# Router exponentials of the last two sequences as powers on GpSimd, and Silu for every expert block

## The chip, the cores and the metric

The kernel runs on one core of a Trainium2 chip. The metric is the device time of one execution in microseconds (us), the median over several runs.

## The reference

The input `x` is 32 sequences of 256 tokens with 128 features. The reference computes an attention layer (16 heads of 64, causal softmax, output projection), adds the input and normalises. Then comes a mixture of 8 experts:

```
xn     = layernorm(x) * gamma + beta
probs  = softmax(xn @ router_w.T / 1.5)        # 8 experts
w, idx = top_k(probs, 2)
h      = silu(xn @ W1[e])                      # 128 -> 512, for the two chosen experts
y      = h @ W2[e]                             # 512 -> 128
out    = layernorm(x + sum over the two of w * y)
```

All of it is float32. `silu(z)` is `z * sigmoid(z)`, which is also `0.5 * z * (tanh(z / 2) + 1)`.

## The kernel before

Each engine has one program, written out by hand in order; an engine takes up an instruction only when the one before it has been taken up, and semaphores join the engines. There is no planner: what is written first runs first.

*Attention* runs in 32 x 4 steps (`step(n, q, d)`; four quads of heads for each sequence). The products with split weights are three matmuls each, with a rounded high part and a low part. During sequence n the kernel also finishes sequence n - 1: projection, residual, norm (on GpSimd, with powers of -0.5 for the square roots, L586 and L597), then the router. One router call is: logits on TensorE, `router_difference` on VectorE (minus the maximum, L1174 and L1176), `router_exponentials` on ScalarE (L804), `router` on VectorE (sum, top 8, index, gates, `chosen`, L1107 to L1137), `ranks` on TensorE, `places` on VectorE, `slots` on GpSimd, and `send_tokens`, four indirect writes of the token rows into a queue in HBM sorted by expert (L639). The calls are numbered 2 to 33. The last two, 32 and 33, no longer fall into attention but among the first expert blocks.

*The experts* run over `NJ` = 71 blocks of 256 queued rows. For block j the SyncE queue loads the rows (`m_x`), TensorE transposes them (L1523), ScalarE applies gamma and beta (`affine`, L887) and rounds (`m_xhi`, L890), VectorE makes the low part (`m_xlo`, L1302), TensorE does the first layer (`hidden`, L1424, into two halves of PSUM), the activation function is applied, TensorE does the second layer (`output`, L1718), VectorE weights the result (`rows`, L1312, two blocks later), and GpSimd writes it to `y_tok` in HBM with two indirect writes (L742). There are 4 buffers for results: `rows(j)` waits until the writes of block j - 4 have landed.

The order within block j on each engine is:

- TensorE: transposes of block j + 1, first layer of block j, extra work (block 4: logits of router 33; block 2: ranks of router 32; block 7: ranks of router 33), second layer of block j - 1.
- ScalarE: `affine(j + 1)`, the two halves of the activation function, the copy of the weights of block j + 2 (L901, L903).
- VectorE: `rows(j - 2)`, `destinations(j)` (five small operations and `m_keep`; L1271 to L1294), `m_xlo` of block j + 1, extra work (block 0: `router(32)`; block 4: `router_difference(33)`; block 6: `router(33)`).
- GpSimd: results of sequence 32 first (norm, slots, `send_tokens`), then the two writes of each block; `slots(33)` and its four queue writes stand in front of block 9.

In blocks 0 to 5 (`SILU_FROM` = 6) ScalarE makes Tanh of half the hidden value, and VectorE makes `(tanh + 1) * z` from it (L1360); the missing factor 0.5 is in the gates. From block 6 on ScalarE makes Silu in one instruction. Tanh and Exp are in one activation table; Silu is in another, and the one load stands in front of block 6's first Silu.

Of the kernel before, what the change touches and what calls it, by code (L numbers as in the profile page):

```python
# [1 line left out]

# [8 lines left out]
ALU = mybir.AluOpType  # L11
# [3 lines left out]
P = 128  # L15
# [7 lines left out]
ROWS = BLOCKS * P  # L23
WBUFS = 4
LATER = 71
SILU_FROM = 6
FBUFS = 6
EARLY = 11
FIRST_LOAD, LOAD_EVERY = 37, 3
# [6 lines left out]
def postln_block(nc, x, wq, wk, wv, bq, bk, bv, wo, bo, gamma, beta, router_wt, w1, w2, out):  # L36
# [37 lines left out]
    with ExitStack() as ctx:  # L74
        def sb(name, shape, dt=F32):
            return ctx.enter_context(nc.sbuf_tensor(name, shape, dt))
# [4 lines left out]
        def sem(name):  # L81
            return ctx.enter_context(nc.semaphore(name))
# [87 lines left out]
        r_negmax = sb("r_negmax", [P, TILES])  # L170
        r_diff = sb("r_diff", [P, TILES, E])
        r_exp = sb("r_exp", [P, TILES, E])
        r_sum = sb("r_sum", [P, TILES])
        r_inv = sb("r_inv", [P, TILES])
        r_top = sb("r_top", [P, TILES, E])
# [46 lines left out]
        m_w2 = sb("m_w2", [P, E * HID])  # L222
        m_xhi = sb("m_xhi", [P, 2, ROWS], F32R)
        m_xlo = sb("m_xlo", [P, 2, ROWS], F32R)
        m_tanh = [early_use[:, at * HD:at * HD + CH * ROWS].rearrange("p (c t) -> p c t", c=CH) for at in (9, 15)]
        m_h = early_use[:, 10 * HD:10 * HD + 2 * CH * ROWS].rearrange("p (a c t) -> p a c t", a=2, c=CH)
        m_xf = early_use[:, 12 * HD:12 * HD + 2 * ROWS].rearrange("p (a t) -> p a t", a=2)
        m_y = early_use[:, 14 * HD:14 * HD + YBUFS * ROWS].rearrange("p (a b d) -> p a b d", a=YBUFS, b=BLOCKS)
# [114 lines left out]
        m_xnt_done = sem("m_xnt_done")  # L343
        m_xhi_done = sem("m_xhi_done")
        m_xlo_done = sem("m_xlo_done")
        m_tanh_done = sem("m_tanh_done")
        m_h_done = sem("m_h_done")
        m_silu_done = sem("m_silu_done")
        m_rows_done = sem("m_rows_done")
        m_second_done = sem("m_second_done")  # L350
# [56 lines left out]

        def wait_units(engine, j, half):

            if j < SILU_FROM:  # L410
                engine.wait_ge(m_h_done, j * 2 + half + 1)
            else:
                engine.wait_ge(m_silu_done, (j - SILU_FROM) * 2 + half + 1)

        def f_sum(f):

# [112 lines left out]
        def _(pool):  # L529
# [7 lines left out]
            for par in range(2):  # L537
                pool.iota(z[:, par, :, TOK], [[P, TILES]], base=(par - 2) * S, channel_multiplier=1,
                          allow_small_or_imprecise_dtypes=True)
            pool.memset(eps_sb[:], EPS)  # L540
            pool.memset(neg_half[:], -0.5)
            pool.memset(neg_one[:], -1.0)
            pool.memset(neg_two[:], -2.0)
# [104 lines left out]
            def residual_input(n):  # L648
# [5 lines left out]
                    ins = pool.tensor_tensor(xb[:, i, :], x_raw[:, (n - 1) % 2, i, :], bo_sb[:], ALU.add)  # L654
                ins.then_inc(xb_done, 1)

            def round_outputs(s):
                m, first = s // QUADS, s % QUADS * 2
                pool.wait_ge(ot_done, s + 1)
                if m >= 1:  # L660
                    pool.wait_ge(out_half_ready, 2 * m - (1 if first < 4 else 0))
                pool.tensor_copy(ot_hi[:, first:first + 2, :], ot[:, s % 2]).then_inc(ot_hi_done, 1)  # L662
# [42 lines left out]
            for s in range(LAST - 2, LAST):  # L705
                round_outputs(s)
                rest_of_outputs(s)
            residual_input(SEQS)
            send_tokens(SEQS - 1, 1)
            norm(SEQS)  # L710
            slots(SEQS)
# [18 lines left out]
            for j in range(NJ):  # L730
                if LATER <= j + 2 < NJ:
                    rest_of_expert_weights(j + 2)
                if j == 9:
                    slots(SEQS + 1)
                    for i in range(TILES):
                        send_tokens(SEQS + 1, i)
                if j - 2 in load_at[:EARLY]:
                    piece_power(load_at.index(j - 2))
                pool.wait_ge(m_dest_done, j + 1)
                pool.wait_ge(m_rows_done, j + 1)  # L740
                for i in range(BLOCKS):
                    pool.indirect_dma_start(  # L742
                        y_tok, bass.IndirectOffsetOnAxis(ap=m_dest[:, j % (2 * YBUFS), i:i + 1], axis=0),
                        m_y[:, j % YBUFS, i, :], None, bounds_check=TOP * TOKENS - 1, oob_is_err=False
                    ).then_inc(m_y_sent[j % YBUFS], 16)
# [11 lines left out]
        def _(act):  # L757
# [146 lines left out]
                ins.then_inc(m_w_hi_done, 1)  # L904

            affine(0)
            copy_outputs(LAST - 2)
            first_pt(LAST)
            expert_weights(0)
            copy_outputs(LAST - 1)  # L910
            expert_weights(1)
            router_exponentials(SEQS)
            for j in range(NJ):
                if 1 <= j < NJ - 1:
                    affine(j + 1)
                for half in range(2):
                    act.wait_ge(m_z_ready, j * 2 + half + 1)
                    if j < SILU_FROM:
                        act.activation(m_tanh[j % 2][:, 2 * half:2 * half + 2, :], hidden_at(j, half), ACT.Tanh, scale=0.5
                                       ).then_inc(m_tanh_done, 1)  # L920
                    else:
                        act.activation(m_h[:, j % 2, 2 * half:2 * half + 2, :], hidden_at(j, half), ACT.Silu
                                       ).then_inc(m_silu_done, 1)
                if j == 0:
                    affine(1)
                if j + 2 < NJ:
                    expert_weights(j + 2)
                if j == 1:
                    copy_projection(SEQS)
                if j == 3:  # L930
                    act.wait_ge(zt_ready, SEQS)
                    act.activation(xnt[:], ps_f[:, 0:S], ACT.Identity, scale=gamma_sb[:, 0:1],
                                   bias=beta_sb[:, 0:1]).then_inc(xnt_done, 1)
                if j == 5:
                    router_exponentials(SEQS + 1)

            for f in range(FINS - EARLY):
                act.wait_ge(f_shift_done, f + 1)
# [7 lines left out]
        def _(dve):  # L946
# [321 lines left out]
            def destinations(j):  # L1268
                dve.wait_ge(m_x_loaded[j % WBUFS], (j // WBUFS + 1) * 16)
                line = m_x[:, j % WBUFS]  # L1270
                dve.scalar_tensor_tensor(out=m_second[:, j % 2, :], in0=line[:, :, SLOT], scalar=t_row[:, j:j + 1],  # L1271
                                         in1=row_no[:], op0=ALU.subtract, op1=ALU.is_equal
                                         ).then_inc(m_second_done, 1)
                dve.wait_ge(m_second_done, j + 1)
                if j >= 2 * YBUFS:
                    dve.wait_ge(m_y_sent[j % YBUFS], (j // YBUFS - 1) * BLOCKS * 16)
                dve.scalar_tensor_tensor(out=m_dest[:, j % (2 * YBUFS), :], in0=m_second[:, j % 2, :], scalar=float(TOKENS),  # L1277
                                         in1=line[:, :, TOK], op0=ALU.mult, op1=ALU.add).then_inc(m_dest_done, 1)
                dve.scalar_tensor_tensor(out=m_scale[:, j % 2, :], in0=m_second[:, j % 2, :], scalar=1.0,
                                         in1=line[:, :, KEEP], op0=ALU.subtract, op1=ALU.mult  # L1280
                                         ).then_inc(m_scale_done, 1)
                if j < SILU_FROM:
                    dve.scalar_tensor_tensor(out=m_extra[:, j % 2, :], in0=m_second[:, j % 2, :], scalar=0.5,
                                             in1=line[:, :, MORE], op0=ALU.mult, op1=ALU.mult).then_inc(m_extra_done, 1)
                else:
                    dve.tensor_tensor(m_extra[:, j % 2, :], m_second[:, j % 2, :], line[:, :, MORE], ALU.mult
                                      ).then_inc(m_extra_done, 1)
                dve.wait_ge(m_scale_done, j + 1)
                for i in range(BLOCKS):
                    ins = dve.tensor_scalar(m_keep[:, j % 3, i, :], line[:, i, 0:D], m_scale[:, j % 2, i:i + 1], None,  # L1290
                                            ALU.mult)
                ins.then_inc(m_keep_done, 1)
                dve.wait_ge(m_extra_done, j + 1)
                dve.scalar_tensor_tensor(out=m_gate[:, j % 4, :], in0=line[:, :, GATE],  # L1294
                                         scalar=0.5 if j < SILU_FROM else 1.0, in1=m_extra[:, j % 2, :],
                                         op0=ALU.mult, op1=ALU.add).then_inc(m_gate_done, 1)

            def rest_of_x(j):
                dve.wait_ge(m_xhi_done, j + 1)
# [50 lines left out]
            for j in range(NJ):  # L1350
# [2 lines left out]
                destinations(j)  # L1353
                if 1 <= j < NJ - 1:
                    rest_of_x(j + 1)
                for half in range(2) if j < SILU_FROM else ():
                    dve.wait_ge(m_tanh_done, j * 2 + half + 1)
                    if j >= 2 and half == 0:
                        dve.wait_ge(m_rows_ready, j - 1)
                    dve.scalar_tensor_tensor(out=m_h[:, j % 2, 2 * half:2 * half + 2, :],  # L1360
                                             in0=m_tanh[j % 2][:, 2 * half:2 * half + 2, :], scalar=1.0,
                                             in1=hidden_at(j, half), op0=ALU.add, op1=ALU.mult
                                             ).then_inc(m_h_done, 1)
                if j == 0:
                    rest_of_x(1)
                if j >= NJ - 2:
                    rows(j - 1)
                if j == 0:
                    router(SEQS)
                if j == 1:  # L1370
                    residual(SEQS)
                    statistics(SEQS)
                    variance(SEQS)
# [458 lines left out]
```

## Time and profile before

| | us |
|---|---|
| median of 3 runs | 1269.91 (1268.1 to 1270.12) |
| the profiled execution | 1270.98 |
| its span, first to last instruction | 1269.2 |
| TensorE matmuls busy | 1244.1 (98%) |
| ScalarE busy | 1117.4 (88%) |
| VectorE busy | 1054.5 (83%) |
| GpSimd busy | 753.3 (59%) |

The shares are averages over the whole span. Attention takes the span up to about 990 us, the expert blocks go on to about 1249, and the last results come to the end. The mean granted TensorE clock is 0.998 of full. A number in square brackets at a line of a timeline is how long the engine was idle before it, and what ended that.

### The profile page before, as it was taken

The numbers are of one execution on the slowest core, as the hardware profiler recorded it, in microseconds if no ns is written. First come the engines' busy times: TensorE is split into PE (matmuls) and PEld (weight loads), VectorE is DVE, ScalarE is ACT, GpSimd is POOL, SyncE is SP. The second block draws the span as 40 slices with busy tenths as digits, with TensorE's granted clock in tenths as the row PEclk, the third lists the DMA queues.
The fourth block names the chain that finished last, engine by engine and source line by source line (L and its number), as shares of the span: only waits on it lengthen the run. The fifth ranks groups of instructions, "written<-read, shape, count | busy, mean of one in ns | idle before, by whom it ended". The sixth has DMA issues, their size and how long they took to land.

```text
span 1269.2 us, 35973 instructions
## 1 busy us (share of the span) xinstructions
PE 1244.1 (98%) x11020; PEld 1112.8 (88%) x11020; DVE 1054.5 (83%) x5231; ACT 1117.4 (88%) x3470; POOL 753.3 (59%) x1325
## 2 busy tenths in 40 slices
PE   7999999999999999999999999999999899999997
PEld 6888888888888888888888888888888799999996
DVE  6888888888888888888888888888889786568885
ACT  7899999999999989999889999888888789999994
POOL 2246666666555555555555555555555777557776
PEclk9999999999999999999999999999999999999999
DMA  5000000000000000000000000000004223244553
GB/s 215 6 14 23 23 23 23 23 23 23 15 15 15 14 17 17 19 16 17 14 15 15 15 14 14 14 15 14 14 15 154 99 85 92 80 116 145 151 169 131
DMA packets 49212, 60.95 MB, mean 48 GB/s; under 512 B 8304, under 2 KB 35059, under 8 KB 48768
## 3 DMA queue, kind: packets, MB, share of 16 engines
q1 hardware_dynamic: 39376, 41.44, 10.5%
q0 software_dynamic: 8640, 17.13, 4.2%
q8 instruction: 92, 1.51, 0.5%
q14 instruction: 96, 0.79, 0.2%
q10 hardware_dynamic: 1008, 0.08, 0.1%
HBM read 30.72 MB, written 28.81 MB: 47 GB/s over the span
## 4 chain that ended last, share of the span: by engine, by line
PE 94%; ACT 2%; DVE 2%; issue 1%; DMA 0%; POOL 0%; SPq 0%; ACTq 0%; POOLq 0%; DVEq 0%
PE ps_a L1424 15%; PE ps_s L1467 13%; PE ps_s L1446 11%; PE ps_s L1424 8%; PE ps_f L1502 7%; PE ps_b L1459 7%; PE ps_f L1459 6%; PE ps_b L1718 5%; PE ps_a L1718 5%; PE ps_s L1449 4%; PE ps_b L1424 4%; PE ps_f L1424 3%; PE ps_a L1523 1%; PE ps_s L1477 1%; ACT f_y L777 1%
## 5 line engine op out<-in xcount | busy, mean ns | idle before, releaser
L777 ACT ACTIVATE f_y<-f_y,neg_max 128x256 f32<-128x256 f32 x512 | 256.4, 501 | 45.6 <-DVE neg_max L1074 45.5
L1074 DVE CUSTOM_DVE_ANT_0 f_y<-ps_s,mask 128x256 f32<-128x256 f32 x512 | 214.5, 419 | 63.5 <-PE ps_s L1449 63.2
L1424 PE MATMUL ps_a<-xt_hi,weights 128*128 128x256 f32 x1024 | 242.8, 300 | 0.0
L667 POOL TENSOR_TENSOR ot_lo<-f_y,ot_hi 128x512 fp32r<-128x512 f32 x128 | 164.8, 1287 | 116.3 <-PE ps_s L1449 111.0
L1090 DVE TENSOR_SCALAR f_y<-f_y,inv_sums 128x256 f32<-128x256 f32 x512 | 194.7, 380 | 6.9
L780 ACT ACTIVATE f_y<-f_y,neg_max 128x128 f32<-128x128 f32 x512 | 199.6, 390 | 0.0
L1467 PE MATMUL ps_s<-ident,f_y 128*128 128x128 f32 x1536 | 195.3, 274 | 0.0
L1424 PEld LDWEIGHTS ps_a<-xt_hi,weights 128*128 128x128 f32 x1024 | 175.7, 189 | 16.0 <-issue 10.8
L742 POOL DMA_INDIRECT y_tok<-f_y,m_dest x142 | 146.3, 1031 | 67.5 <-DVE m_dest L1277 38.1
L1446 PE MATMUL ps_s<-qk 64*128 64x256 f32 x1024 | 176.5, 421 | 5.6 <-ACT pt L825 2.5
L1467 PEld LDWEIGHTS ps_s<-ident,f_y 128*128 128x128 f32 x1536 | 172.2, 141 | 4.9 <-issue 0.5
L1091 DVE TENSOR_SCALAR f_y<-f_y,inv_sums 128x128 f32<-128x128 f32 x512 | 161.3, 315 | 0.0
L639 POOL DMA_INDIRECT queue<-z,slot_now x128 | 128.5, 1004 | 36.0 <-issue 26.4
L1078 DVE CUSTOM_DVE_ANT_0 f_y<-ps_s,mask 128x128 f32<-128x128 f32 x512 | 146.3, 286 | 0.0
L1424 PE MATMUL ps_a<-xt_lo,weights 128*128 128x256 f32 x512 | 144.6, 282 | 0.0
L766 ACT ACTIVATE qk<-ps_a,bq_sb 128x256 f32<-128x256 f32 x256 | 119.2, 466 | 22.6 <-PE ps_a L1424 22.5
L1424 PE MATMUL ps_s<-m_xhi,weights 128*128 128x256 f32 x568 | 117.6, 291 | 3.5 <-DVE m_xlo L1302 2.3
L767 ACT ACTIVATE qk<-ps_a,bk_sb 128x256 f32<-128x256 f32 x256 | 119.4, 467 | 0.0
L662 POOL CAST ot_hi<-f_y 128x512 fp32r<-128x512 f32 x128 | 78.3, 611 | 64.9 <-ACT f_y L810 64.9
L1446 PEld LDWEIGHTS ps_s<-qk 64*128 64x128 f32 x1024 | 77.7, 185 | 38.2 <-issue 27.6
L1449 PEld LDWEIGHTS ps_s<-qk 64*128 64x128 f32 x1024 | 99.8, 187 | 10.8
L1191 DVE COPY pt<-ps_s 128x768 f32<-128x768 f32 x97 | 92.2, 950 | 10.0 <-PE ps_s L1467 10.0
(254 smaller groups left out, 3338.8 us busy)
## 6 DMA issues: line engine op xcount, KB each, us to landing
m_x<-queue SPq DMA_DIRECT2D x71, 133.0 KB, 2.3
f_y<-y_tok SPq DMA_DIRECT2D x32, 256.0 KB, 3.3
queue<-empty SPq DMA_DIRECT2D x8, 532.0 KB
x_raw<-in_x SPq DMA_DIRECT2D x32, 128.0 KB
out_x<-f_y SPq DMA_DIRECT2D x16, 256.0 KB, 3.3
y_tok<-f_y,m_dest POOLq DMA_INDIRECT x142
f_y<-in_w SPq DMA_DIRECT2D x1, 2048.0 KB, 11.3
m_w<-in_w SPq DMA_DIRECT2D x1, 2048.0 KB, 15.2
```

The lines of the kernel that those rows point to most:

```text
L667: pool.tensor_tensor(ot_lo[:, first:first + 2, :], ot[:, s % 2], ot_hi[:, first:first + 2, :].bitcast(F32), ALU.subtract).then_inc(ot_lo_d ...
L742: pool.indirect_dma_start(y_tok, bass.IndirectOffsetOnAxis(ap=m_dest[:, j % (2 * YBUFS), i:i + 1], axis=0), m_y[:, j % YBUFS, i, :], None, ...
L777: act.activation(row[:, 0:2 * P], row[:, 0:2 * P], ACT.Exp, scale=-1.0, bias=neg_max[:, pair, h, 0:1], accum_out=sums[:, d % 2, pair, h, 0:1])
L780: act.activation(row[:, 2 * P:3 * P], row[:, 2 * P:3 * P], ACT.Exp, scale=-1.0, bias=neg_max[:, pair, h, 1:2], accum_out=sums[:, d % 2, pa ...
L1074: dve.tensor_tensor_reduce(out=row[:, 0:2 * P], in0=ps_s[:, pair, h, 0:2 * P], in1=mask[:].rearrange("p a b -> p (a b)"), scale=-1.0, scal ...
L1090: dve.tensor_scalar(row[:, 0:2 * P], row[:, 0:2 * P], inv_sums[:, d % 2, pair, h, 0:1], None, ALU.mult)
L1091: ins = dve.tensor_scalar(row[:, 2 * P:3 * P], row[:, 2 * P:3 * P], inv_sums[:, d % 2, pair, h, 1:2], None, ALU.mult)
L1424: ins = pe.matmul(dst, lhs, rhs, start=(i == 0), stop=(i == len(terms) - 1))
L1446: pe.matmul(ps_s[:, pair, h, 0:2 * P], qk[r, pair, 0, P:2 * P], qk[r, pair, 1, :], start=True, stop=True)
L1449: ins = pe.matmul(ps_s[:, pair, h, 2 * P:3 * P], qk[r, pair, 0, 0:P], qk[r, pair, 1, 0:P], start=False, stop=True, skip_group_check=True)
L1459: ins = pe.matmul(dst_bank[r, cols], v[:, k, c * P + h * DH:c * P + (h + 1) * DH], pt[:, s % 2, pair, h, src], start=(k == 0), stop=(k == ...
L1467: ins = pe.transpose(ps_s[:, pair, h, dst:dst + P], probs[:, buf, pair, h, src:src + P], ident[:])
```

## The change

ScalarE makes Silu in all 71 blocks, straight into `m_h`; the tiles `m_tanh` and VectorE's 12 instructions at L1360 are gone, with the factors of 0.5 in the gates. A Silu over one column (`silu_first`), placed behind `affine(0)`, calls for the Silu table there. Routers 32 and 33 no longer use ScalarE: GpSimd makes `ROUTER_BASE ** r_diff` with `ROUTER_BASE = exp(1 / 1.5)`, as a power of 128x16 elements, from a tile filled at the start. For router 32 this stands behind `residual_input(32)`; for router 33 in block 3, ahead of that block's two writes. VectorE's `router(32)` moves from block 0 to block 1.

```
+ROUTER_BASE = math.exp(1.0 / ROUTER_TEMP)
...
+            pool.memset(router_base[:], ROUTER_BASE)
...
+            def router_powers(n):
+                pool.wait_ge(r_diff_done, n - 1)
+                if n == SEQS:
+                    pool.wait_ge(r_idx_done, n - 2)
+                pool.tensor_tensor(r_exp[:], router_base[:], r_diff[:], ALU.pow).then_inc(r_exp_done, 1)
...
             residual_input(SEQS)
+            router_powers(SEQS)
             send_tokens(SEQS - 1, 1)
             norm(SEQS)
...
             for j in range(NJ):
                 if LATER <= j + 2 < NJ:
                     rest_of_expert_weights(j + 2)
+                if j == 3:
+                    router_powers(SEQS + 1)
                 if j == 9:
                     slots(SEQS + 1)
...
             affine(0)
+            act.activation(silu_first[:], eps_sb[:, 0:1], ACT.Silu)
             copy_outputs(LAST - 2)
             first_pt(LAST)
             expert_weights(0)
             copy_outputs(LAST - 1)
             expert_weights(1)
-            router_exponentials(SEQS)
...
-                    if j < SILU_FROM:
-                        act.activation(m_tanh[j % 2][:, 2 * half:2 * half + 2, :], hidden_at(j, half), ACT.Tanh, scale=0.5
-                                       ).then_inc(m_tanh_done, 1)
-                    else:
-                        act.activation(m_h[:, j % 2, 2 * half:2 * half + 2, :], hidden_at(j, half), ACT.Silu
-                                       ).then_inc(m_silu_done, 1)
+                    act.activation(m_h[:, j % 2, 2 * half:2 * half + 2, :], hidden_at(j, half), ACT.Silu
+                                   ).then_inc(m_silu_done, 1)
...
-                if j == 5:
-                    router_exponentials(SEQS + 1)
...
-                for half in range(2) if j < SILU_FROM else ():
-                    dve.wait_ge(m_tanh_done, j * 2 + half + 1)
-                    if j >= 2 and half == 0:
-                        dve.wait_ge(m_rows_ready, j - 1)
-                    dve.scalar_tensor_tensor(out=m_h[:, j % 2, 2 * half:2 * half + 2, :],
-                                             in0=m_tanh[j % 2][:, 2 * half:2 * half + 2, :], scalar=1.0,
-                                             in1=hidden_at(j, half), op0=ALU.add, op1=ALU.mult
-                                             ).then_inc(m_h_done, 1)
...
-                if j == 0:
+                if j == 1:
                     router(SEQS)
-                if j == 1:
                     residual(SEQS)
```

## Rows read from the trace of the kernel before

**Rows 1.** The page's chain that ended last, shares of the span by engine.
```profile
PE 94%; ACT 2%; DVE 2%; issue 1%; DMA 0%; POOL 0%; SPq 0%; ACTq 0%; POOLq 0%; DVEq 0%
```

**Rows 2.** Windows: stretch, its us, each engine's busy us, granted clock, DMA.
```profile
1003.40:1026.20 22.80, 22.80 (x204) 22.79 (x205) 17.47 (x79) 19.88 (x40) 14.48 (x31) 1.00 0.22 59
1026.20:1033.00 6.80, 4.99 (x47) 4.73 (x46) 6.19 (x41) 5.34 (x11) 5.16 (x6) 1.00 0.22 70
991.00:992.00 1.00, 1.00 (x10) 0.81 (x8) 0.94 (x2) 0.56 (x2) 0.92 (x4) 0.50 0.09 16
```

**Rows 3.** Timeline of TensorE: start, us taken, instructions, idle before and releaser.
```profile
990.03 0.51 PE L1523 MATMUL ps_a<-ident,m_x 128*128 128x128 f32 x2 [2.26 <-DMA m_x<-queue]
990.47 2.83 PE L1459 MATMUL ps_b<-pt,f_y 128*64 128x256 f32 x16
...
997.39 1.52 PE L1459 MATMUL ps_b<-pt,f_y 128*64 128x256 f32 x16
...
1028.30 0.36 PE L1424 MATMUL ps_s<-m_xhi,weights 128*128 128x256 f32 x1 [1.81 <-DVE m_xlo L1302]
```

**Rows 4.** The chain in order of time, behind block 7's first layer: start, us.
```profile
1029.95 0.02 PE ps_f L1483
...
1032.18 1.42 PE ps_s L1424 x12
```

**Rows 5.** Timeline of VectorE.
```profile
996.81 1.25 DVE L1277 SCALAR_TENSOR_TENSOR m_dest<-m_second,m_x 128x2 int32<-128x2 f32 x1
...
1002.77 0.42 DVE L1302 TENSOR_TENSOR m_xlo<-f_y,m_xhi 128x256 fp32r<-128x256 f32 x1
...
1026.12 0.61 DVE L1312 SCALAR_TENSOR_TENSOR f_y<-ps_b,m_gate,f_y 128x128 f32<-128x128 f32 x2 [3.50 <-issue]
...
1027.96 0.16 DVE L1107 TENSOR_REDUCE r_sum<-r_exp 128x2 f32<-128x16 f32 x1
...
1029.34 0.19 DVE L1137 TENSOR_TENSOR chosen_any<-chosen 128x16 bf16<-128x16 f32 x1
...
1031.06 0.41 DVE L1302 TENSOR_TENSOR m_xlo<-f_y,m_xhi 128x256 fp32r<-128x256 f32 x1
...
1145.59 0.16 DVE L1277 SCALAR_TENSOR_TENSOR m_dest<-m_second,m_x 128x2 int32<-128x2 f32 x1
```

**Rows 6.** Timeline of GpSimd.
```profile
996.76 1.27 POOL L667 TENSOR_TENSOR ot_lo<-f_y,ot_hi 128x512 fp32r<-128x512 f32 x1
...
1001.56 0.86 POOL L654 TENSOR_TENSOR xb<-x_raw,bo_sb 128x128 f32<-128x128 f32 x2
...
1009.80 0.19 POOL L582 TENSOR_SCALAR ln_b<-mv 128x2 f32<-128x2 f32 x1 [4.94 <-DVE mv L1158]
...
1022.87 0.99 POOL L742 DMA_INDIRECT y_tok<-f_y,m_dest  x1 [0.30 <-issue]
...
1028.03 0.98 POOL L742 DMA_INDIRECT y_tok<-f_y,m_dest  x1 [0.30 <-issue]
...
1145.11 1.07 POOL L720 TENSOR_TENSOR g_r<-g_a,neg_half 128x4 f32<-128x4 f32 x1
```

**Rows 7.** Timeline of ScalarE.
```profile
993.34 0.60 ACT L810 ACTIVATE f_y<-ps_b 128x512 f32<-128x512 f32 x1 [1.75 <-PE ps_b L1459]
...
1024.16 1.28 ACT L922 ACT_TABLE_LOAD   x1
1025.46 1.09 ACT L922 ACTIVATE f_y<-ps_s 128x512 f32<-128x512 f32 x2
```

**Rows 8.** Groups by line and shape: count, busy us, mean ns of one, idle before.
```profile
L597 POOL TENSOR_TENSOR ln_r<-ln_a,neg_half 128x2 f32<-128x2 f32 x32 | 22.0, 686 | 0.0
L752 POOL TENSOR_TENSOR f_r<-f_a,neg_half 128x4 f32<-128x4 f32 x5 | 5.1, 1018 | 3.7 <-DVE f_a L1417 3.1 <-ACT f_y L941 0.4
L612 POOL TENSOR_TENSOR slot_four<-slot_part 128x16 f32<-128x16 f32 x32 | 8.3, 259 | 2.5
L1360 DVE SCALAR_TENSOR_TENSOR f_y<-f_y,ps_s 128x512 f32<-128x512 f32 x12 | 7.7, 679 | 2.7 <-ACT f_y L919 2.7
```

More of the change, by code:

```diff
@@ L1 @@
+import math
 from contextlib import ExitStack
@@ L25 @@
 LATER = 71
-SILU_FROM = 6
+ROUTER_BASE = math.exp(1.0 / ROUTER_TEMP)
 FBUFS = 6
@@ L172, in postln_block @@
         r_exp = sb("r_exp", [P, TILES, E])
+        router_base = sb("router_base", [P, TILES, E])
+        silu_first = sb("silu_first", [P, 1])
         r_sum = sb("r_sum", [P, TILES])
@@ L224, in postln_block @@
         m_xlo = sb("m_xlo", [P, 2, ROWS], F32R)
-        m_tanh = [early_use[:, at * HD:at * HD + CH * ROWS].rearrange("p (c t) -> p c t", c=CH) for at in (9, 15)]
         m_h = early_use[:, 10 * HD:10 * HD + 2 * CH * ROWS].rearrange("p (a c t) -> p a c t", a=2, c=CH)
@@ L345, in postln_block @@
         m_xlo_done = sem("m_xlo_done")
-        m_tanh_done = sem("m_tanh_done")
-        m_h_done = sem("m_h_done")
         m_silu_done = sem("m_silu_done")
@@ L408, in wait_units @@
         def wait_units(engine, j, half):
-            if j < SILU_FROM:
-                engine.wait_ge(m_h_done, j * 2 + half + 1)
-            else:
-                engine.wait_ge(m_silu_done, (j - SILU_FROM) * 2 + half + 1)
+            engine.wait_ge(m_silu_done, j * 2 + half + 1)
         def f_sum(f):
@@ L917, in _ @@
                     act.wait_ge(m_z_ready, j * 2 + half + 1)
-                    if j < SILU_FROM:
-                        act.activation(m_tanh[j % 2][:, 2 * half:2 * half + 2, :], hidden_at(j, half), ACT.Tanh, scale=0.5
-                                       ).then_inc(m_tanh_done, 1)
-                    else:
-                        act.activation(m_h[:, j % 2, 2 * half:2 * half + 2, :], hidden_at(j, half), ACT.Silu
-                                       ).then_inc(m_silu_done, 1)
+                    act.activation(m_h[:, j % 2, 2 * half:2 * half + 2, :], hidden_at(j, half), ACT.Silu
+                                   ).then_inc(m_silu_done, 1)
                 if j == 0:
@@ L1281, in destinations @@
                                          ).then_inc(m_scale_done, 1)
[L1282 to L1287, printed above, removed]
+                dve.tensor_tensor(m_extra[:, j % 2, :], m_second[:, j % 2, :], line[:, :, MORE], ALU.mult
+                                  ).then_inc(m_extra_done, 1)
                 dve.wait_ge(m_scale_done, j + 1)
@@ L1293, in destinations @@
                 dve.wait_ge(m_extra_done, j + 1)
-                dve.scalar_tensor_tensor(out=m_gate[:, j % 4, :], in0=line[:, :, GATE],
-                                         scalar=0.5 if j < SILU_FROM else 1.0, in1=m_extra[:, j % 2, :],
-                                         op0=ALU.mult, op1=ALU.add).then_inc(m_gate_done, 1)
+                dve.tensor_tensor(m_gate[:, j % 4, :], line[:, :, GATE], m_extra[:, j % 2, :], ALU.add
+                                  ).then_inc(m_gate_done, 1)
             def rest_of_x(j):
```

## The prediction

> **What bounds the kernel now.** I read the page's chain first: 94% of the time to the end lies on TensorE [rows 1]. An edit elsewhere pays only where TensorE stands still, so I went to the stretch that the diff touches, from the end of attention to expert block 8. The table of windows [rows 2] says where it stands still: in 1003.40 to 1026.20, blocks 1 to 6, TensorE is busy for all 22.80 us; in 1026.20 to 1033.00 for only 4.99 of 6.80. Then the timelines of the engines. TensorE starts block 7's first layer at 1028.30 after 1.81 us of idle, behind `m_xlo` [rows 3]. VectorE made that late because it had stood still for 3.50 us before L1312 at 1026.12, and no engine's work is named as what ended it [rows 5]. What came last is the landing of a `y_tok` write: the result rows of block 4 reuse the buffer of block 0, whose second write GpSimd only starts at 1022.87 and leaves at 1023.86 [rows 6]; 2.2 us more is 1026.1. GpSimd is the late engine here: the norm, the slots and the queue writes of sequence 32 come after 1009.80, the block results behind them, 1.29 us from write to write (four from 1022.87 to 1028.03). The place in that queue decides what the change costs.
>
> **Part by part.** Routers 32 and 33 are the last two calls (n = 32 and 33).
>
> 1. *Silu in place of Tanh in blocks 0 to 5.* On VectorE 12 instructions of 679 ns go, 8.1 us [rows 8]. They stood beside a TensorE that had no idle time in blocks 1 to 6 to give back, and in block 6, where VectorE does hold TensorE up, it waits for a landing; an earlier idle engine meets the same landing. Worth 0. On ScalarE two Silu of one block take 1.09 us [rows 7]; should Tanh be a tenth cheaper, ScalarE's idle time in blocks 1 to 6 (19.88 busy of 22.80) takes it: 0. The gate's 128x2 operations only change form: 0.
>
> 2. *The table load.* It leaves 1024.16, where it takes 1.28 us and Silu follows 1.30 after its start, and goes behind `affine(0)`, ahead of a ScalarE idle time of 1.75 us that ends at 993.34 [rows 7]. Load plus a one-column Silu, which I price as a plain small operation, 0.2 (below the 0.26 of rows 8), is 1.5: it fits with 0.25 to spare. Were there no gap it would cost its 1.5, so that is the upper end. I take 0. Its going out of block 6 gives 0 too: there TensorE waits for `m_xlo`, which needs nothing of that Silu.
>    The row shows 1.30 us from load to use. The Trainium skill, page "ScalarE: Activation LUTs", section "What ACT_TABLE_LOAD costs", puts a switch at about 2.66 us, with a drain. By that the load overruns the gap by 1.1 us (an estimate) and the end is up to that much later; this trace disagrees with the drain.
>
> 3. *Small pieces.* The first exponential leaves ScalarE's queue just before block 0's activations, on the way to block 1: a gain. The memset of `router_base` stands in GpSimd's start, ahead of everything: a loss. Each lies between 0 and the 0.26 us of a plain 16-column operation [rows 8]; I take 0.1 for each, and they cancel. The second exponential stood where nobody waited: 0.
>
> 4. *What a power of 16 columns costs.* The trace has none. A power of 2 columns takes 686 ns, of 4 columns 1018, where a plain operation on 16 takes 259 [rows 8]. Two more columns cost 0.33 us, 0.166 each: 1.02 + 12 x 0.166 = 3.0 us. Ends: 1.07, the 4-column power of rows 6, if the price is per instruction; and 4.2 if all of the 2-column price above a plain operation grows with the columns ((0.69 - 0.19) / 2 x 16 + 0.2, with a plain one estimated at 0.19). I take 3.0: two widths show a price per column.
>
> 5. *Router 32.* GpSimd reaches this power behind `residual_input`, at 1001.56 + 0.86 = 1002.42, and ends it at 1005.4. Its norm waited 4.94 us until 1009.80 for VectorE [rows 6], and the two queue writes before it have room to move by 3.0. On VectorE the router now stands in block 1, is over some 1.6 us after the power, near 1007, and the norm's input still comes at its old time because it waits for a projection on TensorE. Worth 0, up to a power of 4.9 us.
>
> 6. *Router 33, the one that costs.* Here the power stands in front of block 3's writes. It can start when block 2's second write ends, 1028.03 + 0.98 = 1029.01 [rows 6], and ends at 1032.0. VectorE comes to the router at 1027.96 [rows 5] and found the exponentials ready; now it waits 4.1 us, and behind it queue the result rows of block 5 and `m_xlo` of block 8. The router runs from 1027.96 to 1029.34 + 0.19 = 1029.53, that is 1.57, so the choice is there at 1032.04 + 1.57 = 1033.6. TensorE's ranks of router 33 stand between block 7's first layer and block 6's second, and ran at 1029.95 [rows 4]; they now wait until 1033.62, that is 3.67 us. `m_xlo` of block 8 ends 1.9 us behind the choice (1029.53 to 1031.47 [rows 5]), at 1035.6, and TensorE wants it 2.23 us behind the ranks (1029.95 to 1032.18 [rows 4]), at 1035.9: no second wait. The writes from block 3 on go out 3.0 us later and TensorE runs 3.67 later, so no landing comes late that did not before; slots 33 in block 9 move along. What follows is TensorE's and moves as one.
>
> 7. *The clock.* The idle of 2.26 us before 990.03 was followed by the lower level, 0.50 of full in 991 to 992, and 16 matmuls that take 1.52 us at the upper took 2.83 [rows 2, 3]. The idle of 1.81 was followed by none: 1.00 up to 1033.00 [rows 2]. The new idle of 3.67 is longer than the one that brought the fall, and comes 1.65 us of work after the one of 1.81. I take one fall at that row's price, 2.83 - 1.52 = 1.3.
>
> Sum: 0.1 - 0.1 + 3.67 + 1.3 = 5.0 us. The profiled execution took 1270.98, so 1276.0 on its own scale; it lies 1.07 over the median of the runs, 1269.91, on which the forecast is 1274.9.
>
> **A shared port.** From 996.76 GpSimd runs a 128x512 subtraction for 1.27 us, and VectorE's 128x2 `m_dest`, 0.16 at 1145.59, takes 1.25 inside it at 996.81. But that 0.16 at 1145.59 lies under a power, 1145.11 to 1146.18 [rows 5, 6]. The Trainium skill, page "SBUF — State Buffer", section "SBUF: two separate sides", lets GpSimd and VectorE have one pair of ports in turn, for the whole instruction, where VectorE reads two SBUF inputs. By that rule a power would hold VectorE as the subtraction did; the first pair of rows agrees, the second does not. The rival that this makes is priced below from rows.
>
> **Rivals.** A measurement of this kernel can tell about 0.2% (2.5 us) from no change.
>
> - *The stall of step 6, but no fall of the clock*, chance 0.24: the idle of 1.81 brought none. 1269.91 + 3.7 = 1273.6, slower.
> - *A power priced by the instruction*, 1.07 us, 0.15. For it: a plain operation on 16 columns costs only 259 ns. Against it: the two widths of powers. The choice is there at 1029.01 + 1.07 + 0.04 + 1.57 = 1031.69, the ranks wait 1.74, the clock holds as it did after 1.81: 1271.6, within the bound.
> - *The first power holds VectorE's port*, 0.09: 16 columns may read for longer than 4 did. `m_xlo` of block 1 has two SBUF inputs and started at 1002.77, inside 1002.42 to 1005.42; it would end at 1005.84 instead of 1003.19, and TensorE waits for it with nothing between: 2.65 more, 1277.5.
> - *The faster side*, 0.06: VectorE's backlog and not GpSimd's sets blocks 0 to 7, the idle of 3.50 being put down wrongly. Then the 8.1 us freed give back the 1.81 before block 7: 1268.1, and up to 1.5 more at block 1, where VectorE's work ahead of `m_xlo` also ended close to it: 1266.6. It decides from the point where router 33's power ends by 1027.96; by the rows it can't start before 1029.01, so GpSimd's queue would have to be 4 us earlier, and I see nothing that moves it by more than tenths.
> - By the skill's price of a table switch (step 2) the end would be up to 1.1 later, 1276.0; chance 0.03, counted as slower.
>
> **Numbers.** The forecast with all its terms has the rest, 0.43. Slower by over 0.2%: 0.43 + 0.24 + 0.09 + 0.03, less 0.04 because 3.7 us is near the bound: 0.75. Within 0.2%: 0.15 + 0.04 = 0.19. Faster: 0.06. The range goes from the cheap power, 1271.4 with a little for the runs' scatter, to the held port, 1277.4; a power of 4.2 us (1276.1) lies inside.
>
> **What would show it.** GpSimd has two powers of about 3.0 us, near 1002.4 and 1029.0. VectorE is idle some 4 us before L1107 of router 33, TensorE 3.7 us before the ranks behind block 7, and then a window at 0.50. The idle of 1.81 before block 7 stays, ScalarE's gap before 993.3 holds the load, and nothing changes behind block 9 but the hour. The forecast is wrong if the second power takes under 2 us, if VectorE doesn't wait at router 33, or if `m_xlo` of block 1 takes longer than 0.5 us.

## The result and the profile after

The changed kernel took 1278.66 us (median of 4 runs, 1276.29 to 1279.72), the kernel before beside it 1270.01 (4 runs). The ratio is 1.0068 [1.0056, 1.0081]: slower, and above the upper end of the forecast's range, 1277.4. Two repeats in later groups gave 1277.17 and 1277.73. Over all runs of the study the changed kernel stands at 1277.64 (15 runs), 0.2 above the range, and the kernel before at 1271.00 (64 runs), 6.6 us apart; the forecast had 5.0.

The profiled execution took 1276.29, its span 1274.5. First the page's busy times and chain of the changed kernel; the chain answers to [rows 1].

```profile
PE 1245.6 (98%) x11020; PEld 1114.3 (87%) x11020; DVE 1048.2 (82%) x5219; ACT 1117.5 (88%) x3469; POOL 757.4 (59%) x1328
...
PE 93%; ACT 2%; DVE 2%; POOL 1%; issue 1%; DMA 0%; SPq 0%; ACTq 0%; POOLq 0%; DVEq 0%
```

GpSimd has come into the chain with 1%. The waits of TensorE from 1000 to 1070 say where (line, tile, who ended the wait: us in total, times, longest). First the changed kernel, then the kernel before.

```profile
PE ps_f L1470 <- DVE chosen_any L1138: 3.8, 1, 3.8
PE ps_s L1411 <- DVE m_xlo L1298: 2.3, 2, 1.8
PE ps_a L1510 <- ACT f_y L894: 0.9, 1, 0.9
```

```profile
PE ps_s L1424 <- DVE m_xlo L1302: 2.3, 2, 1.8
PE ps_a L1523 <- ACT f_y L887: 1.0, 1, 1.0
```

One wait of 3.8 us is new, all others are the old ones. Its three links, in the timelines of TensorE, VectorE and GpSimd of the changed kernel (start, us, instruction, idle before and who ended it):

```profile
1027.81 0.36 PE L1411 MATMUL ps_s<-m_xhi,weights 128*128 128x256 f32 x1 [1.85 <-DVE m_xlo L1298]
...
1033.28 0.17 PE L1470 MATMUL ps_f<-chosen_any,before_bf 128*128 128x8 bf16 x1 [3.83 <-DVE chosen_any L1138]
```

```profile
1002.21 0.42 DVE L1298 TENSOR_TENSOR m_xlo<-f_y,m_xhi 128x256 fp32r<-128x256 f32 x1 [3.90 <-ACT m_xhi L897]
...
1002.80 0.16 DVE L1278 SCALAR_TENSOR_TENSOR m_dest<-m_second,m_x 128x2 int32<-128x2 f32 x1
...
1031.42 0.17 DVE L1108 TENSOR_REDUCE r_sum<-r_exp 128x2 f32<-128x16 f32 x1 [3.86 <-POOL r_exp L659]
...
1032.92 0.22 DVE L1138 TENSOR_TENSOR chosen_any<-chosen 128x16 bf16<-128x16 f32 x1
```

```profile
1001.93 2.94 POOL L659 TENSOR_TENSOR r_exp<-router_base,r_diff 128x16 f32<-128x16 f32 x1
...
1009.23 0.19 POOL L580 TENSOR_SCALAR ln_b<-mv 128x2 f32<-128x2 f32 x1 [1.85 <-DVE mv L1159]
...
1027.35 1.07 POOL L749 DMA_INDIRECT y_tok<-f_y,m_dest  x1 [0.30 <-issue]
1028.42 2.97 POOL L659 TENSOR_TENSOR r_exp<-router_base,r_diff 128x16 f32<-128x16 f32 x1
```

GpSimd reaches the second power only when block 2's second write is over and works on it for 2.97 us; VectorE stands still for 3.86 us before the router; TensorE, behind it, waits 3.83 us for the choice. The idle of 1.81 before block 7 [rows 3] stays, as 1.85. Then the clock, in the windows and the chain of the changed kernel (in a window: start and end, its us, busy us of TensorE's matmul and weight load, VectorE, ScalarE, GpSimd, granted clock, DMA share and GB/s):

```profile
1033.00:1034.00 1.00, 0.72 (x9) 0.71 (x10) 0.96 (x6) 0.00 (x0) 0.91 (x1) 0.99 0.19 66
1034.00:1036.00 2.00, 2.00 (x11) 2.00 (x11) 1.23 (x9) 0.00 (x0) 1.48 (x2) 0.50 0.19 66
...
1037.00:1038.00 1.00, 1.00 (x9) 1.00 (x8) 0.96 (x7) 0.64 (x2) 0.76 (x1) 0.80 0.42 133
```

```profile
1033.55 3.32 PE ps_b L1705 x16
1036.87 0.43 PE ps_a L1510 x2
1037.29 1.52 PE ps_s L1411 x12
1038.81 1.78 PE ps_a L1705 x16
```

The level falls to 0.50 (1.2 GHz) at about 1034.0, 0.7 us after TensorE resumed at 1033.28, and is back at 1037.4. TensorE is busy all through these 3.4 us, so all of them cost. A second layer takes 3.32 in it and 1.78 behind it.

To see what a stall costs in all I cut each profiled run at two instructions that every kernel has: the two transposes at the end of attention (L1673 before, L1660 after; 987.37 and 986.99) and the first rank matmul of router 33.

| profiled run | transposes to ranks | ranks to the end of the span |
|---|---|---|
| before | 42.42 | 239.41 |
| changed | 46.29 | 241.22 |
| changed, second profile | 46.03 | 241.27 |
| changed, third profile | 45.76 | 242.36 |

The first column holds the wait, 3.3 to 3.9 over the kernel before; the second the clock, 1.8 to 2.95 over it. The expert blocks themselves keep their pace in all four profiles, 3.41 us each.

### The profile page after: what moved, and what is told of

Its sections match the earlier page's. It is cut to its first block, busy times and chain, and to the rows that moved or that the text cites. A ratio compares the mean times of both kernels' runs of the same rounds, so it can differ in the third digit from the quotient of the medians.

```text
span 1274.5 us, 35960 instructions
## 1 busy us (share of the span) xinstructions
PE 1245.6 (98%) x11020; PEld 1114.3 (87%) x11020; DVE 1048.2 (82%) x5219; ACT 1117.5 (88%) x3469; POOL 757.4 (59%) x1328
## 4 chain that ended last, share of the span: by engine, by line
PE 93%; ACT 2%; DVE 2%; POOL 1%; issue 1%; DMA 0%; SPq 0%; ACTq 0%; POOLq 0%; DVEq 0%
PE ps_a L1411 15%; PE ps_s L1454 13%; PE ps_s L1433 11%; PE ps_s L1411 8%; PE ps_f L1489 7%; PE ps_b L1446 7%; PE ps_f L1446 6%; PE ps_b L1705 5%; PE ps_a L1705 5%; PE ps_s L1436 4%; PE ps_b L1411 4%; PE ps_f L1411 3%; PE ps_a L1510 1%; PE ps_s L1464 1%; ACT f_y L784 1%
```

## The experiments

Twelve kernels ran, in three groups of four, each against the kernel before in the same group.

**The changed kernel again**, no edit, once in the first group and once in the second.

> The changed kernel once more, five rounds. The profile of it explained +5.3 us of span (power of 2.97 us, TensorE idle 3.83, one fall of the clock), but the median of the runs moved by 8.65. Theory A (the clock): the extra 3.4 us is TensorE at its lower level for more stretches than in the profiled run; then a run's time goes with its mean granted clock, with about 1276 us where the clock is 0.995 or higher and 1278 to 1280 where it is 0.991 to 0.993, and the kernel before stays at 0.997 or more in most runs. Theory B (the stall itself is longer in most runs, by late writes or a slower power): times of 1278 and more at a clock of 0.995 as well. Median expected 1278.5 by both.

> The changed kernel a third time, beside the others of this group. Theory A (the stall of 3.8 us plus falls of the clock whose number changes from run to run): +5.5 to +8.5 over the kernel before, and the profile again with 46.0 to 46.5 us from the transposes behind attention (L1660) to the ranks of router 33, and 241 to 243 from there to the end. Theory B (the stall itself varies): more than 47 us to the ranks.

They took 1277.17 (5 runs), ratio 1.0049 [1.0036, 1.0062], and 1277.73 (6 runs), 1.0055 [1.004, 1.007]. The new wait was there in both profiles, 4.06 us in the second and 3.62 in the third. The low level lasted as long in the second as in the first, but not in the third:

```profile
1028.00:1030.00 2.00, 1.85 (x12) 1.58 (x12) 0.00 (x0) 0.65 (x2) 2.00 (x2) 0.84 0.24 67
1030.00:1033.00 3.00, 0.00 (x0) 0.00 (x0) 1.22 (x12) 1.70 (x3) 2.69 (x2) 0.50 0.09 26
1033.00:1036.00 3.00, 2.46 (x15) 2.46 (x16) 2.42 (x15) 0.00 (x0) 2.20 (x3) 0.50 0.13 44
1036.00:1039.00 3.00, 3.00 (x16) 3.00 (x15) 1.39 (x8) 0.96 (x2) 2.39 (x3) 0.50 0.39 111
1039.00:1042.00 3.00, 3.00 (x27) 3.00 (x25) 2.00 (x10) 2.36 (x5) 2.26 (x3) 0.90 0.26 76
```

The low level lasts about 10.2 us, from 1029.4 to 1039.6; it begins behind the idle time of 1.89 before block 7, lies partly on the stall, where it costs nothing, and costs 2.95 by the table. One stall of one program has more than one price.

**Powers taken out.** In place of both powers ScalarE does a copy of the same size at the old places of its exponentials. This kernel leaves the exponentials out, so the gates of these 512 tokens are other numbers; `router(32)` stays in block 1.

```diff
-            router_powers(SEQS)          # GpSimd, both calls go
+            act.activation(r_exp[:], r_diff[:], ACT.Copy, scale=1.0 / ROUTER_TEMP).then_inc(r_exp_done, 1)   # ScalarE
```

> Silu in all blocks and the table load at the end of attention as in the changed kernel, but no power on GpSimd: ScalarE copies the router differences (scaled) in place of the exponentials of the last two routers, at the places of the kernel before. The experts chosen stay the same, the gates of these 512 tokens are other numbers, which is the part left out. Theory A (only the power at router 33 costs; Silu, the 12 instructions taken from VectorE and the moved load are worth nothing): 1270 us, within 1 of the kernel before, the idle time of 1.8 us before block 7 unchanged. Rival (VectorE's backlog mattered): 1268 or less, with that idle time gone. Rival (the moved table load costs in most runs): 1271.5 or more.

1271.22 (12 runs) against 1271.31, ratio 0.9999 [0.9991, 1.0008]. TensorE's waits in 1000 to 1070 of this kernel:

```profile
PE ps_s L1416 <- DVE m_xlo L1303: 2.1, 2, 1.6
PE ps_a L1515 <- ACT f_y L895: 1.0, 1, 1.0
```

They are those of the kernel before, to 0.2 us. So Silu, the 12 VectorE instructions that go and the table load at its new place are together worth nothing that these runs resolve (the interval is about 1 us to either side), and all of the loss hangs on the powers.

**The powers alone**, on the kernel before, in the places that they have in the changed kernel, with `router(32)` in block 1; Tanh and VectorE's twelve instructions stay.

```diff
+            router_powers(SEQS)          # before send_tokens(SEQS - 1, 1), and SEQS + 1 before block 3
-            router_exponentials(SEQS)    # ScalarE, both calls go
```

> The kernel before (Tanh and VectorE's 12 instructions in blocks 0 to 5, table load in block 6), with only the two exponentials moved to GpSimd as powers and router 32 in block 1. Theory A: the whole loss is here, the same 1278 to 1279 as the changed kernel (+8 to +9), with TensorE idle 3.8 us before the ranks of router 33. If the Silu part took or gave a share, this differs from the changed kernel by more than 1 us.

1278.64 (5 runs), 1.0059 [1.0046, 1.0072]. The ranks wait 3.80, and the level is at 0.50 for 3.4 us behind it. This kernel takes 1.5 us more than the changed kernel beside it (1277.17), and two windows show where: the same stretch of 130 us in the middle of the expert blocks, first of the changed kernel, then of this one.

```profile
1100.00:1230.00 130.00, 130.00 (x1144) 130.00 (x1144) 96.75 (x495) 118.77 (x230) 86.35 (x84) 1.00 0.46 133
```

```profile
1100.00:1230.00 130.00, 130.00 (x1138) 130.00 (x1137) 96.31 (x493) 119.20 (x229) 87.50 (x84) 1.00 0.45 130
```

TensorE is busy throughout, at the full clock, and gets through six matmuls fewer. A block takes 3.433 us in place of 3.413 (38 blocks by their transposes), some 1.2 us over the 62 blocks behind the ranks. With that taken off, the powers alone cost what the whole change costs. Why the pace differs is open.

**The power twice.** A second one into a spare tile, ahead of that of router 33.

```diff
+                if n == SEQS + 1:
+                    pool.tensor_tensor(r_spare[:], router_base[:], r_diff[:], ALU.pow)
                 pool.tensor_tensor(r_exp[:], router_base[:], r_diff[:], ALU.pow).then_inc(r_exp_done, 1)
```

> The changed kernel with a second power of 128x16 (into a spare tile) in front of router 33's own, so that GpSimd is 2.98 us later with the exponentials. Theory A: TensorE waits 3.83 + 2.98 = 6.8 us before the ranks, 49.0 to 49.5 us from the transposes behind attention to the ranks, and the time is that of the changed kernel plus 3.0 (1280 to 1281.5), plus or minus one step of the clock. Rival (later work takes the delay up): less than +2.

1282.94 (4 runs), 1.0091 [1.0076, 1.0105]: 11.9 us over the kernel before, where the changed kernel had 6.6. GpSimd's timeline, then TensorE's:

```profile
1029.60 2.97 POOL L661 TENSOR_TENSOR r_spare<-router_base,r_diff 128x16 f32<-128x16 f32 x1
1032.52 2.92 POOL L662 TENSOR_TENSOR r_exp<-router_base,r_diff 128x16 f32<-128x16 f32 x1
```

```profile
1037.32 0.17 PE L1473 MATMUL ps_f<-chosen_any,before_bf 128*128 128x8 bf16 x1 [6.65 <-DVE chosen_any L1141]
```

The wait grows by 2.82, so the power stands on the path with nearly all of its length. But the time lies above the 1280 to 1281.5 that was expected. This kernel too runs its blocks slower, 3.447 us, which is 2.0 over 60 blocks; with the 2.82 that leaves 0.5 of the 5.3. The clock accounts for about that much: its low level lasts from 1035.0 to 1041.8, so 4.5 us of it lie on work where the changed kernel had 3.4.

**The power one block earlier**, before block 2's writes.

```diff
-                if j == 3:
+                if j == 2:
                     router_powers(SEQS + 1)
```

> The changed kernel with the power of router 33 one block earlier in GpSimd's queue, in front of block 2's writes: it starts at 1025.8 and ends at 1028.7. Theory A: VectorE waits 1.2 us, TensorE 1.1 to 1.3 before the ranks in place of 3.8, 43.5 to 43.9 us to the ranks, block 2's later writes stop nobody, and 3 to 4.5 us less than the changed kernel (a wait of 1.2 should bring the clock down less often): 1272 to 1274.5. Rival (the writes of block 2, 3 us later, hold VectorE's rows of block 6): a wait of VectorE at L1308 in block 8 and no more than 2 us won.

1273.2 (12 runs), 1.0018 [1.0009, 1.0026], 2.2 over the 1271.0 beside it. Its waits of TensorE in 1000 to 1070, and a window:

```profile
PE ps_s L1411 <- DVE m_xlo L1298: 3.3, 3, 1.9
PE ps_f L1470 <- DVE chosen_any L1138: 1.1, 1, 1.1
```

```profile
1030.00:1033.00 3.00, 2.48 (x25) 2.47 (x26) 2.57 (x16) 1.20 (x3) 2.23 (x3) 1.00 0.14 47
```

Two writes fewer ahead of the power (2.6 us) take 2.7 off the wait, and the clock holds. A third `m_xlo` wait, of 0.95 at 1061.53, is new; VectorE had stood 3.81 us ahead of its rows there, as it does ahead of block 7 [rows 5]. 1.10 and 0.95 make 2.05 of the 2.2 measured: here, where the clock holds, the waits add up to the loss.

**TensorE kept busy in the waits**, by matmuls of `ident` into a free corner of PSUM ahead of block 7's first layer and ahead of the ranks: 14 and 28 of them, then 7 and 16.

```diff
+                if j == 7:
+                    pe.wait_ge(r_diff_done, SEQS)
+                    keep_clock(ps_f[:, 0:P], 7)     # 14 in the first kernel
...
                     pe.wait_ge(r_diff_done, SEQS)
+                    keep_clock(ps_f[:, 0:P], 16)    # 28 in the first kernel
                     pe.wait_ge(chosen_any_done, SEQS)
```

> The changed kernel with dummy matmuls of 128x128 on TensorE in its two waits: 14 before block 7's first layer, 28 before the ranks of router 33 (some 1.5 and 3.1 us, inside idle times of 1.85 and 3.83 us). They take away the idle TensorE, not the wait. Theory A: no fall of the clock around 1033, and a time of the kernel before plus the bare wait, 1270.0 + 3.7 = 1273.7 (1273 to 1275), with less scatter than the changed kernel's. Theory B: the runs stay at 1277 to 1278 whatever the clock does, at most 1.6 us less than the changed kernel.

> The fillers of the kernel before this one in the same waits, cut to 7 and 16 (a filler took 0.22 us and not 0.11, so that 14 and 28 overran both waits by 1.5 and 2.5 us). Now 1.5 and 3.5 us, inside the waits of 1.85 and 3.83. Theory A: no fall at 1033; from the ranks to the end 239.4 to 239.9 us as in the kernel before, against 241.2 of the changed kernel, so 1.6 us less than the changed kernel run beside it, and +3.8 over the kernel before. Theory B: no gain, within 0.5 of the changed kernel.

The first missed, by the size of its filler. One call is two instructions and took 0.23 us, so 28 calls outran the wait (TensorE's timeline, first the longer kernel, then the shorter):

```profile
1032.09 6.41 PE L1668 MATMUL ps_f<-ident 128*128 128x128 f32 x56
```

```profile
1027.86 3.73 PE L1668 MATMUL ps_f<-ident 128*128 128x128 f32 x32
1031.93 0.18 PE L1470 MATMUL ps_f<-chosen_any,before_bf 128*128 128x8 bf16 x1 [0.35 <-DVE chosen_any L1138]
```

It took 1279.12, 1.0061 [1.0048, 1.0074]. The shorter one fits and took 1276.12 (6 runs), 1.0046 [1.0031, 1.0061]. Its profile has no fall at either place, and from the ranks to the end it needs 240.27, 1.0 to 2.1 less than the three profiles of the changed kernel. The longer kernel's profile has no fall at the ranks either (239.85 to the end), whereas all six profiles with an unfilled stall there (3.62 to 6.65 us) have one. A caution: the shorter kernel's profile shows no fall behind the idle time of 2.34 at the end of attention either, where nothing was filled, so the filler is not the only thing that can keep a fall away. Over the runs the filler is worth 1.6 us against the 1277.73 beside it, but the intervals overlap: the clock's price is shown in the profiles, in the runs only as likely. And the median stands 5.8 over the kernel before, where the bare wait of 3.8 was expected. The profiled execution, 1273.95, was the fastest of the six, so what the others lost in addition is not known.

**Eight result buffers.** `y_tok`'s source blocks no longer reuse the buffer of four blocks ago.

```diff
-YBUFS = 4
+YBUFS = 8
```

> The changed kernel with 8 buffers for block results instead of 4, so that VectorE's rows of block 4 don't wait for the write of block 0; the power of router 33 stays in front of block 3's writes. Theory A (GpSimd's queue fixes the time of the power): the idle time before block 7 (1.5 to 1.85) goes, VectorE waits at router 33 that much longer, the ranks come at the same distance, 46.0 to 46.5 us, and the time is the changed kernel's within 0.7. Rival (the two waits of TensorE add up and are independent): 1.8 us less than the changed kernel.

1277.66 (6 runs), 1.0051 [1.0036, 1.0066], the same as the changed kernel. TensorE's and VectorE's waits here:

```profile
PE ps_f L1470 <- DVE chosen_any L1138: 5.8, 1, 5.8
PE ps_a L1510 <- ACT f_y L894: 0.9, 1, 0.9
PE ps_s L1411 <- DVE m_xlo L1298: 0.5, 1, 0.5
```

```profile
1032.75 0.17 DVE L1108 TENSOR_REDUCE r_sum<-r_exp 128x2 f32<-128x16 f32 x1 [6.99 <-POOL r_exp L659]
```

The 1.8 before block 7 is gone, and 2.0 come back at the ranks. GpSimd's queue pins the time of the choice; what TensorE gains ahead of it, it waits for there. That the 1.8 goes with the buffers also confirms the prediction's reading of it, a wait for the landing of an earlier result.

**The power ahead of all block writes**, on top of the eight buffers.

```diff
-                if j == 3:
+                if j == 0:
                     router_powers(SEQS + 1)
```

> Eight buffers, and the power of router 33 in front of block 0's writes, where GpSimd stands at about 1020.6 and the differences have been there since 1017.5; it ends at 1023.6, VectorE comes to router 33 at about 1024. Theory A: neither wait is left; 40.5 us from the transposes to the ranks, no fall behind them, and 1.5 to 2.0 us less than the kernel before. Rival (the writes of block results that now go out 3 us later stop VectorE elsewhere, at 8 blocks' distance or before the pieces of the end are loaded): the kernel before within 0.5, or slower.

1272.23 (12 runs), 1.0012 [1.0, 1.0025]. The new wait and the 1.81 are both gone, and the expected gain did not come. TensorE's and GpSimd's timelines:

```profile
1060.33 0.57 PE L1510 MATMUL ps_a<-ident,m_x 128*128 128x128 f32 x2 [2.35 <-DMA m_x<-queue]
```

```profile
1021.67 3.14 POOL L659 TENSOR_TENSOR r_exp<-router_base,r_diff 128x16 f32<-128x16 f32 x1
...
1054.73 0.95 POOL L637 DMA_INDIRECT queue<-z,slot_now  x1 [0.30 <-issue]
```

GpSimd's last write of sequence 33 into the queue goes out at 1054.73; a block fetched behind it arrives 2.35 us late, and the clock is at 0.50 from 1060.5 to 1063.9 behind it. The power's 3 us have moved to the next deadline of the same engine.

**The slots of router 33 ahead too**, before block 4 in place of block 9.

```diff
-                if j == 9:
+                if j == 4:
                     slots(SEQS + 1)
```

> Eight result buffers, the power of router 33 in front of block 0's writes, and slots 33 with its four queue writes in front of block 4's writes instead of block 9's. In the kernel without this last move TensorE stood still 2.35 us at 1060.3 for the rows of block 17, which wait for the queue writes of sequence 33, done at 1055.7; now they are done near 1042. Theory A: no wait of TensorE behind block 1 is left, 40.6 us to the ranks, 239.4 from there, and 1.5 to 2.5 us less than the kernel before. Rival (VectorE stands at rows of block 12 for the writes of block 4, 7.4 us later): the kernel before within 0.7.

1268.31 (8 runs), 0.9975 [0.9965, 0.9985]: faster than both kernels, by 2.7 us than the one before. That is 0.2 more than the most that was expected. TensorE is busy throughout its windows:

```profile
1003.40:1026.20 22.80, 22.80 (x206) 22.79 (x205) 15.02 (x90) 19.55 (x40) 18.10 (x31) 1.00 0.21 54
1026.20:1033.00 6.80, 6.80 (x66) 6.75 (x64) 5.01 (x29) 6.21 (x12) 5.28 (x6) 1.00 0.30 88
1033.00:1070.00 37.00, 37.00 (x327) 37.00 (x326) 26.50 (x130) 33.62 (x66) 28.57 (x36) 1.00 0.32 89
```

From the transposes to the ranks it takes 40.15, 2.3 less than the kernel before: the 1.81 is given back, and some tenths more. Whether the kernel before with eight buffers and early slots, without any power, does as well was not run.

**The idle at the end of attention filled as well**, 8 calls there on top of the last kernel.

```diff
+                        keep_clock(ps_a[:, 0, 0:P], 8)
                         transpose_x(0)
```

> The kernel of the last expectation, with 8 dummy matmuls (1.76 us) on TensorE in its 2.2 us wait for the first rows at 988. Theory A of the clock: the fall at 990 goes, in which 16 matmuls took 2.83 instead of 1.52 us, so 1.0 to 1.7 us less than without them and 3 to 4 less than the kernel before. Rival (the slow matmuls there wait for the loads of weights anyway): no difference over 0.5.

Median 1268.24 of 12 runs, no gain; with one run at 1281.63, whose mean clock was 0.947, the interval is 0.999 [0.997, 1.0009]. The fall at 990 is gone, but one stands at 996.5 instead (windows, first without, then with the filler):

```profile
990.00:991.00 1.00, 1.00 (x4) 0.52 (x6) 1.00 (x2) 0.33 (x1) 0.92 (x2) 0.50 0.37 99
...
996.00:1000.00 4.00, 3.78 (x34) 3.22 (x35) 2.61 (x10) 1.41 (x4) 2.60 (x4) 1.00 0.05 17
```

```profile
990.00:993.00 3.00, 2.62 (x26) 1.84 (x25) 2.57 (x4) 1.93 (x3) 2.79 (x6) 1.00 0.35 98
996.00:1000.00 4.00, 4.00 (x24) 2.69 (x25) 1.46 (x5) 0.23 (x1) 2.70 (x3) 0.57 0.24 67
```

That the filler moved it is not shown: in the kernel with the power ahead of all block writes, whose idle time of 2.17 there is not filled, the fall stands at 995.7 to 999.1 as well, and in the third profile of the changed kernel at 991.8.

## Why the prediction was right in its mechanism and wrong in its number

- *Steps 1 and 2, at 0: right.* Without the powers the change measures 0.9999 [0.9991, 1.0008]. ScalarE's timeline of the changed kernel around the load:

```profile
991.34 1.28 ACT L914 ACT_TABLE_LOAD   x1
992.64 0.20 ACT L914 ACTIVATE silu_first<-eps_sb 128x1 f32<-128x1 f32 x1
993.08 0.60 ACT L817 ACTIVATE f_y<-ps_b 128x512 f32<-128x512 f32 x1 [0.24 <-PE ps_b L1446]
```

  Load and first Silu took 1.50 from start to end, and 0.24 of the gap was left, where 1.5 and 0.25 were forecast. The drain that the Trainium skill, page "ScalarE: Activation LUTs", section "What ACT_TABLE_LOAD costs", adds to a switch does not show: Silu starts 1.30 after the load does. That rival fell.
- *Step 3: not told apart*; the pieces lie below what the runs resolve.
- *Step 4, the power at 3.0: right.* 2.94 and 2.97 us. From 4 columns (1018 ns, [rows 8]) to 16 it is 0.163 a column. The rival priced by the instruction fell.
- *Step 5, router 32 at 0: right.* The power ran from 1001.93, the norm still waited 1.85 of its 4.94 [rows 6], and its start came no later.
- *Step 6, 3.67: right*, 3.83 in the profile. The router's chain took 1.72 where 1.57 was forecast, and that is the difference. The two repeats had 4.06 and 3.62. The wait of VectorE was 3.86 for 4.1. No second wait came behind it.
- *Step 7, one fall at 1.3: this step failed, by its size.* The fall was forecast, and it came, but cost 1.8, 1.9 and 2.95. The row that I took the price from [rows 3] shows sixteen matmuls, behind which ScalarE's work was due [rows 7], and I priced those sixteen alone. At the ranks the fall lay on a full second layer and the first layer behind it: 1.5 on the sixteen matmuls, 0.2 on the two transposes, 0.1 on the twelve behind them. And I counted one fall of that length, where the third profile has one three times as long. So the step's wait and its fall were right, and the price of the fall was 0.5 to 1.65 too small. Mean times of the runs, pooled by the mean clock of a run (the first four runs of the kernel before come without a clock):

| mean clock | changed kernel, us (runs) | kernel before, us (runs) |
|---|---|---|
| 0.991 | 1279.43 (3) | |
| 0.993 | 1277.96 (3) | 1273.97 (3) |
| 0.994 | 1278.39 (2) | 1272.90 (1) |
| 0.995 | 1276.85 (5) | 1271.54 (2) |
| 0.996 | | 1272.02 (13) |
| 0.997 | | 1270.95 (18) |
| 0.998 | 1276.45 (2) | 1269.71 (17) |
| 0.999 | | 1269.56 (6) |

  The first four runs of the changed kernel stood at 0.991 to 0.995. The times do go with the clock, but the table does not price the fall: at 0.998 the kernels still stand 6.7 apart, 2.9 more than the wait, in two unprofiled runs of the changed kernel. What they lost there is open.
- *The base.* The three runs shown had a median of 1269.91; sixty-four have 1271.00. I set the forecast on the median of three, against my own profiled execution. On its own scale the forecast was 1276.0, and the profiled execution of the changed kernel took 1276.29. That this is so near is in part luck: 0.2 more wait and 0.5 more clock were offset by attention, which happened to end 0.38 earlier in that execution (986.99 against 987.37).
- *The miss in numbers.* 1277.64 (15 runs) less 1274.9 is 2.7: 1.1 from the base, 1.6 from the sum, of which the first profile shows 0.2 in the wait and the three profiles 0.5 to 1.65 in the clock. The first median lies 1.0 higher still, which I put down to the scatter of the clock; that is argued, not shown.
- *The rival of the held port: fell.* `m_xlo` of block 1 started at 1002.21, inside the first power, and took 0.42, as in [rows 5]; `m_dest` took 0.16 inside it. The rule of the Trainium skill, page "SBUF — State Buffer", section "SBUF: two separate sides", that GpSimd and a VectorE instruction with two SBUF inputs take the pair of ports in turn, each for its whole instruction, is not borne out under a power, though `m_scale`, a 128x2 operation as short, took 1.25 at 996.48 beside a 128x512 subtraction. (By the sum in the prediction this rival ends at 1277.5; the range was closed at 1277.4. Nothing hangs on the 0.1.)
- *The faster side: fell.* VectorE's freed 8.1 us gave nothing (the kernel without powers), and the idle before block 7 went only with the eight buffers.

## What to carry to other kernels

Price an operation that is added to an engine by that engine's next deadlines, not by its busy share: GpSimd was 59% busy, and a 3-us instruction in three places of its queue brought TensorE waits of 3.8, 2.05 or 2.35 us. They were gone only when there were eight buffers and the queue writes behind it had been brought forward too. A new idle of the engine on the critical path is worth its length plus a fall of the clock that varies from run to run, so give it a range and not the price of one row. A median of three runs can be off by 1 us where single runs of the same kernel lie between 1268.1 and 1274.7.

## What was not expected of the hardware

- Two kernels that differ from the others in no instruction of the blocks' TensorE work ran these at 3.433 and 3.447 us a block in place of 3.413, at the full clock and with TensorE busy throughout. The cause is open.
- A fall of the clock can begin while TensorE still works (third profile: 0.84 in 1028 to 1030, with 1.85 of 2.00 us busy, after the idle of 1.9 ahead of block 7) and outlast the stall by six us of full work. In the other two profiles of the same program the level held until about 1034.
- The fall does not come at a fixed place. Behind the idle time of 2.0 to 2.4 us at the end of attention, which nearly every kernel here has, it began between 989.5 and 992.1, once at 995.7 and once not at all. In the one kernel that filled this idle time it stood at 996.5, with no gain in time.
- At the ranks six unfilled stalls had the fall, and two filled ones did not have it.
